# The load of the next x tile is issued at head eleven of the sync engine's loop, not at head fifteen

## The reference

```python
x = x + attn(layernorm(x), Wq, Wk, Wv, Wo)                 # per token: 16 heads attend to the 16 heads of the same token
x = x + xattn(layernorm(x), ctx, Wq, bq, Wkv, bkv, Wp, bp) # all 2048 queries against all 2048 context tokens
x = x + moe(layernorm(x), gate, bias, w1, w2, w3, shared)  # top 2 of 8 experts and a shared one

# xattn, 16 heads of 16 features, q, k, v and the probabilities rounded to 8-bit steps
attn = softmax(q @ k.T)            # (16, 2048, 2048)
out = fq_unsigned(attn) @ v        # (16, 2048, 16), then @ Wp + bp
```

## Time and profile before

| | |
|---|---|
| time, median of 3 runs | 1064.87 us (1064.81 to 1065.13) |
| time of the profiled execution | 1068.14 us |
| its span, first to last instruction | 1065.7 us |
| DVE busy | 906.5 us, 85% |
| POOL, ACT, PE busy | 746.9, 737.3, 722.0 us |
| DVE idle until an x load landed | 40.2 us in 14 waits |
| granted TensorE clock, mean | 0.838 of full speed |

### The profile page before, as it was taken

The page is one execution under the profiler, slowest core; times in us unless marked ns, Lnnn a source line. Parts: engine busy times, 40 slices in busy tenths (PEclk is TensorE's granted clock), DMA queues, the critical chain, the costliest instruction groups (busy, mean ns, idle before and its releaser), DMA issues. The chain is left out here.

```text
span 1065.7 us, 21210 instructions
## 1 busy us (share of the span) xinstructions
PE 722.0 (68%) x7072; PEld 388.6 (36%) x7072; DVE 906.5 (85%) x1841; ACT 737.3 (69%) x989; POOL 746.9 (70%) x728
## 2 busy tenths in 40 slices
PE   6966647666675867675776758576667767675674
PEld 4543323333342524343332425243333324242333
DVE  3887769989888899989898989899888989999851
ACT  2644656868677776868686877778686868878742
POOL 6688987787786778787886868787878868730000
PEclk9975777888896978889897989888878979798965
DMA  6012767979698896979797999979697979999981
GB/s 225 1 40 70 133 119 140 186 115 192 128 176 147 150 173 127 187 114 198 120 194 144 160 168 146 190 121 188 129 179 115 192 150 169 172 167 182 162 161 25
DMA packets 574019, 156.01 MB, mean 146 GB/s; under 512 B 567252, under 2 KB 571863, under 8 KB 573527
## 3 DMA queue, kind: packets, MB, share of 16 engines
q1 hardware_dynamic: 573910, 154.67, 81.5%
HBM read 9.93 MB, written 2.10 MB: 11 GB/s over the span
## 5 line engine op out<-in xcount | busy, mean ns | idle before, releaser
L1135 DVE TENSOR_SCALAR_CACHE_REDUCE score<-ps_score,q_neg 128x1024 f32<-128x1024 f32 x512 | 636.2, 1277 | 17.2 <-PE ps_score L1459 15.9
L824 ACT ACTIVATE prob<-score,exp_bias 128x2048 uint16<-128x2048 f32 x256 | 512.1, 2001 | 61.4 <-DVE exp_bias L1145 58.5
L1459 PE MATMUL ps_score<-keys,queries 128*128 128x512 bf16 x1024 | 368.1, 450 | 255.4 <-DVE score L1135 248.7
L1459 PEld LDWEIGHTS ps_score<-keys,queries 128*128 128x128 bf16 x1024 | 72.2, 103 | 445.7 <-DVE score L1135 415.9
L527 POOL TENSOR_TENSOR product<-hs_exp,v_tok 128x1024 f32<-128x1024 f32 x64 | 149.4, 2347 | 31.0 <-ACT hs_exp L789 30.8
L534 POOL TENSOR_TENSOR product<-product 128x512 f32<-128x512 f32 x128 | 159.5, 1262 | 0.0
L527 POOL TENSOR_TENSOR product<-qk_rot 128x1024 f32<-128x1024 f32 x64 | 150.2, 2349 | 0.3 <-POOL qk_rot L520 0.2
L1489 PE MATMUL ps_pv<-prob_t,values 128*32 128x128 f16 x4096 | 74.2, 229 | 25.1 <-DMA prob_t<-prob 24.8
L545 POOL TENSOR_TENSOR product<-product 128x512 f32<-128x512 f32 x64 | 80.8, 1271 | 5.9 <-POOL product L534 5.9
L1489 PEld LDWEIGHTS ps_pv<-prob_t,values 128*32 128x32 f16 x4096 | 63.2, 101 | 55.2 <-issue 55.2
L466 POOL TENSOR_SCALAR var_eps<-mean_var 128x1 f32<-128x1 f32 x48 | 12.6, 262 | 90.2 <-DVE mean_var L1080 89.2
(11 more groups left out here) (124 smaller groups left out, 1112.2 us busy)
## 6 DMA issues: line engine op xcount, KB each, us to landing
prob_t<-prob SPq DMA_TRANSPOSE x256, 4.5
prob_t<-in_w SPq DMA_DIRECT2D x3, 1024.0 KB, 4.8
x_in<-in_x SPq DMA_DIRECT2D x16, 128.0 KB, 3.0
score<-in_cond_t SPq DMA_DIRECT2D x4, 512.0 KB, 6.3
out<-x_out SPq DMA_DIRECT2D x16, 128.0 KB, 2.7
w_qkv<-in_w_qkv SPq DMA_DIRECT2D x1, 768.0 KB, 4.4
early<-in_w_kv SPq DMA_DIRECT2D x1, 512.0 KB
w_s<-in_w_s SPq DMA_DIRECT2D x3, 128.0 KB
```

What stands on the lines that cost most here:

```text
L824: act.activation(prob[:, s, :].bitcast(U16), score[:, s, :], ACT.Exp, bias=exp_bias[:, s:s + 1], scale=-1.0, accum_out=prob_sum[:, t.par, ...
L1135: dve.tensor_scalar(score[:, s, HALF * i:HALF * i + HALF], ps_score[:, score_slot(t.count(H, h), i)].rearrange("p b k -> p (b k)"), q_neg[ ...
L1459: mm = pe.matmul(ps_score[:, score_slot(n, i), b, :], queries[:, t.par, h // 2, h % 2, :], keys[:, h // 2, k0:k0 + KEYS], start=True, stop ...
```

## The change

SP's loop issues `load_x(t + 3)` ahead of the turn of head 11 in place of head 15. The load, its buffer, its wait for `one_done` and the other engines' lists are as they were.

```diff
                 for h in range(H):
                     if (t + -1).exists() and h == 13:
                         turn_routed(t + -1)
-                    if (t + 3).exists() and h == 15:
+                    if (t + 3).exists() and h == 11:
                         load_x(t + 3)
                     if t.exists() and by_dma(h):
                         turn(h, t)
```

## The result

The changed kernel takes 1031.2 us (median of 4 runs, 1029.04 to 1034.12) beside 1064.84 us before (median of 4, 1062.73 to 1065.13): a ratio of 0.969, 95% interval 0.966 to 0.972. Measured again with five runs, it gave 0.9697 (0.9673 to 0.9721). The forecast was 1030 us.

A forecast was written before the change was run, and what follows sets the result against it. DVE's work and its waits were taken to bound each step. Removing 37.4 us of x waits, less 1.3, 0.2 and 1.2, gave 34.7 us off the 1064.87 median: 1030 us, eight-in-ten range 1023 to 1044.

The forecast's parts named there:

- The wait for x: DVE's waits ahead of L1075 for the x load would vanish: 37.4 us in 13 loop waits, 2.88 us each.
- L884 behind it: At DVE's L1185, which needs ACT's L884: 0.1 us per step taken off the gain, 1.3 us in all.
- The load's own wait: load_x's wait for one_done of tile X-2: met in every step, 12.9 us before SP gets there; nothing queues.
- The layer norm's slack: Between ACT's L760 and PE's L1322: slack falls from 2.75 to 0.6 us; 0.2 us charged in all.
- The push on SP's queue: Load delays turns 11 to 14 and routing transpose: 0.2 us lost in half of 12 steps, 1.2 us.
- The DMA engines: Same bytes, moved between turns 10 and 11: no cost; ring order could cost 0.37 us per step, 4.8 in all.
- Rival B: Part of the gain returns as longer waits at head 8 or the layer norm: 1048 us, 1037 to 1060; chance 0.14.
- The other wait: DVE's wait at head 8 for PE's L1424, 27.4 us in 15: untouched, with 6.5 us either way allowed.
- The sum: Whole kernel: 37.4 - 1.3 - 0.2 - 1.2 = 34.7 us gained, giving 1030 us and a step of 55.3.

The follow-up runs named there:

- the late load: Load of x moved from head 15 to head 0 of the next step in the kernel before: 1094.4 us, ratio 1.0298.
- head 5: Load of x moved from head 15 to head 5 (head 11 in step 0) in the kernel before: 1052.96 us, ratio 0.9907.
- head 13: Load of x moved from head 15 to head 13 in the kernel before: 1029.97 us, ratio 0.9686.
- Relieving POOL: POOL's spread_sums moved behind the layer norm of x, on top of head 13: 1032.8 us, ratio 0.9711 to the kernel before.
- The spare copy: Unused 64 KB load added at head 11 of the kernel before, x still loaded at head 15: 1065.53 us, ratio 1.0016.
- head 14: Load of x moved from head 15 to head 14 in the kernel before: 1032.28 us, ratio 0.9709.
- the later store: Output store moved behind the turn of head 3, on top of head 13: 1014.28 us, ratio 0.9538 to the kernel before.
- three new orders on POOL: spread_sums behind the norm on head 13, then with the later store, then also the norm ahead of a 2.35 us product: 1032.8, 1018.25, 1021.84 us.

## Why the prediction was right, step by step

**The wait for x: right.** Its 37.4 us vanished, and the late load showed the same rule from the other side, 31.5 us of wait for 30.2 us of time.

**L884 behind it: the right neighbour, but it cost nothing.** I took off 0.1 per step, 1.3 us in all. From the start of L1152 to that of L1185 I had worked out 0.69 us (514.01 to 514.7). It is 0.62 at the start of step 13 (832.68 to 833.30) and in seven more of the twelve steps, and 0.45 in the other four, such as the one in the rows above. Without its wait the row before had 3.27 - 2.67 = 0.60. No step shows DVE waiting for L884 there, so this term of the sum measured about nothing.

**The load's own wait: right,** and head 5 shows what it costs where it is not met.

**The layer norm's slack: right in kind.** PE's L1322 is reached with 0.6 us of slack by my sum. In the step after 497.70, L760 ends at 506.55 and PE starts at 507.57, 1.0; over the twelve steps it is 0.05 to 1.1, and PE's waits for L760 there come to 0.1 us. With head 13 the slack is 0.06 in the step shown. Relieving POOL there gave nothing, so the 0.2 us charged was enough.

**The push on SP's queue: the mechanism right, its place only half.** I expected a loss where SP is behind, as in step 9, and none in steps like 6. The largest losses in the trace are in step 8 (0.84 us) and its like, where the turn of head 11 itself took longer (2.42 us in step 6, 1.92 before) and the routing transpose, issued at 488.75, let PE start only at 495.24, 6.5 us later; the median for a turn to land on the profile's page is 4.6. The term was 1.2 us. The spare copy measured 1.7 (0.3 to 3.2). The waits for scores grew by 1.2 in the whole span, but by 2.4 in the twelve steps, and with head 13 and head 14 they are back at 1.3 and 0.8. So the push probably costs about twice what was charged; the 4.8 us in the kernel before with the store moved alone, where no load goes out early, show that this wait also changes for other reasons.

**The DMA engines: right to put at nothing, and the share was no ground for doubt.** Rival B leaned on a DMA share of 0.95. Around the three longest waits at head 8 before, the same column goes above one:

```profile
303.70:307.00 3.30, 3.30 (x68) 2.83 (x57) 0.22 (x2) 2.91 (x5) 2.94 (x2) 0.50 1.13 211
365.20:368.40 3.20, 3.20 (x48) 2.65 (x38) 0.00 (x0) 2.57 (x5) 2.63 (x2) 0.50 1.12 123
774.80:778.00 3.20, 3.20 (x60) 2.72 (x52) 0.68 (x2) 3.20 (x5) 3.20 (x2) 0.50 1.15 217
```

The columns are those of the earlier trace rows; the last but one is the share. A share of 1.13 cannot be occupancy. It is the sum of the times of all packets, and these overlap: in this trace more than 16 packets are in flight on the 16 engines for over half of the span, and up to 31 at once. Of the estimate of 0.37 us per step by ring order no run shows the whole. The spare copy of half the size cost 0.13 us per step (0.02 to 0.25), SP's time included.

**The other wait: its width was right.** The column ahead of the share, the granted clock, is 0.50 in all three rows. These windows hold PE's products of L1489 and L1317 ahead of L1424, at 1.2 GHz. In the first, PE had idled 1.59 us for the transpose of head 3:

```profile
303.52 1.83 PE L1489 MATMUL ps_pv<-prob_t,values 128*32 128x128 f16 x64 [1.59 <-DMA prob_t<-prob]
305.28 1.99 PE L1317 MATMUL ps<-w_o,ho_t 128*128 128x256 f32 x4
```

At 2.4 GHz the two take 1.08 and 1.13 us. Together that is 1.6 us, the larger part of the step from a wait of 1.5 to one of 3.8. It strikes some steps in some executions, so the sum of this wait is 21.3 to 29.0 us over kernels that differ in nothing near it. I had allowed 6.5 us either way. The length of PE's idle time does not decide it by itself: with head 13 PE idled 1.75 us in one step and the products still ran at full clock, and in other profiles 0.72 to 0.94 us went ahead of the lower one. But every wait for L1424 above 2.4 us, in all 14 profiles, has the lower clock under it. Leaving out the first step of the loop, which has the lower clock in every profile and a wait of only 0.8 to 1.3 us, these are 26 of 140 waits with the store ahead of the turn of head 3 and 2 of 56 with it behind that turn, where PE idles about 0.1 us in most steps and not 0.9. At 1.6 us each this may be part of what the later store gave. It is argued from one execution per kernel, and not shown.

**The sum.** 34.7 us were forecast, 33.6 measured. The step was to fall by 2.7 and fell by 2.79. No step that the forecast rests on failed: nearly the whole of it is the 37.4 us of waits, and they went as said. That it came within about 1 us is in part luck. The 1.3 us charged for L884 did not appear and the push seems to have cost 1 us or so more than its 1.2, two errors of opposite sign, and both are smaller than the spread of single executions.

## What to carry to other kernels

A transfer that the bounding engine waits for in every step was worth nearly its wait here, 33.6 of 37.4 us, and moving its issue ahead cost only what it pushed back in the issuing queue. Issue it just early enough to cover the slowest landing, behind the transfers that are more urgent, and never so early that its own buffer wait is unmet: three heads ahead of that release, two thirds of the gain were lost here. When the wait is gone, look at the next one in the list before polishing an engine that merely has no slack: the store moved by one head gave 15.7 us on top of head 13, while none of three new orders on POOL gained anything. But measure each change alone as well: without the early load the same store gave 6 to 7 us. And a wait in one profile is not yet its worth: the profiled executions here lie up to 3 us from their medians.

## What the runs showed of the hardware

The DMA share of a window of about 3 us went to 1.12 to 1.15, and of one of 10 us to 1.22, with up to 31 packets in flight on 16 engines, so a share near one does not show that the engines are full. The granted clock was 0.5 over the head 8 products in three steps of the kernel before and 1.0 in others, and those three steps are some 2 us longer. Those products take 1.6 us more at the lower clock. Behind the first step of the loop it struck them 26 of 140 times where PE had mostly idled 0.9 us or more ahead of them, and 2 of 56 times where it had mostly idled about 0.1. One plain copy of 64 KB in each of 13 steps, among transposes of 512 KB, cost 0.13 us a step by the ratio (0.02 to 0.25).
